# Row clearing, expert weight splitting and the order of the routing work in a four-part transformer block

## The reference

```python
x = x + matmul(fake_quant(norm(x)), fake_quant(ctx))          # 8-bit
x = x + ffn(norm(x))      # 1376 wide; weights rounded in blocks of 32 to 4 bits, activations to 16 bits
x = x + attention(norm(x), ctx)   # 32 query heads, 8 key/value heads of 128; RMS norm on q and k
x = x + moe(norm(x))
```

```python
# moe: 16 experts of 128, two chosen per token, and a shared one of 256
scores = softmax(x @ router_w + router_b) + router_bias
best two groups of four experts, then the best two experts in them; gate = their scores
y  = sum over experts: gate * ((silu(x @ w1 + b1) * (x @ w2 + b2)) @ w3 + b3)
y += (silu(x @ sw1 + sb1) * (x @ sw2 + sb2)) @ sw3 + sb3
```

## Time and profile before

| | |
|---|---|
| Median of 3 runs | 811.12 us (808.1 to 814.69) |
| The profiled execution | 807.26 us, of which the span is 805.4 us |
| PE busy | 647.5 us (80% of the span) |
| DVE | 626.9 us (78%) |
| POOL | 531.1 us (66%) |
| ACT | 494.0 us (61%) |
| Granted TensorE clock, mean | 0.93 of full speed |
| DMA moved | 120.12 MB, mean 149 GB/s |

### The profile page before, as it was taken

How to read it: one execution, slowest core, us unless ns; L and a number is a source line. 1 busy time by engine, 2 the same in 40 slices (tenths; PEclk the granted TensorE clock), 3 DMA queues, 4 the chain that set the end, 5 groups by cost and what they waited for, 6 DMA issues and landing times.

```text
span 805.4 us, 12660 instructions
## 1 busy us (share of the span) xinstructions
PE 647.5 (80%) x3432; PEld 316.6 (39%) x3432; DVE 626.9 (78%) x1331; ACT 494.0 (61%) x986; POOL 531.1 (66%) x505
## 2 busy tenths in 40 slices
PE   0595898846395996999999999999999868676870
PEld 0242343312132442444444444444444335254650
DVE  6896687788899678788888888888888876476622
ACT  4564665659757437777777777777777763145430
POOL 1897586887666557788788888888888744405004
PEclk9899999988688898999999999999999988888995
DMA  8326999992434315877766667666645670499944
GB/s 342 103 81 83 188 188 202 178 166 53 92 59 93 123 58 146 179 169 180 181 142 143 149 156 156 156 143 143 143 92 104 109 244 1 138 289 271 218 145 157
DMA packets 231272, 120.12 MB, mean 149 GB/s; under 512 B 213933, under 2 KB 214189, under 8 KB 228286
## 3 DMA queue, kind: packets, MB, share of 16 engines
q1 hardware_dynamic: 229950, 115.42, 63.3%
q0 software_dynamic: 1280, 4.20, 1.6%
HBM read 57.97 MB, written 15.20 MB: 91 GB/s over the span
## 4 chain that ended last, share of the span: by engine, by line
PE 49%; DVE 20%; DMA 9%; issue 8%; POOL 7%; ACT 4%; SPq 2%; POOLq 0%; DVEq 0%; ACTq 0%
PE ps L1166 16%; PE ps L1168 15%; PE ps L1167 15%; DVE arena L1541 5%; DVE arena L1544 4%; DMA arena<-arena 3%; ACT arena L822 3%; DVE arena L1538 2%; DMA y_d<-arena 2%; POOL arena L594 1%; PE ps L1334 1%; DMA arena<-in_moe_w 1%; POOL arena L586 1%; DVE ss L1691 1%; DMA arena<-in_ffn_w 1%
## 5 line engine op out<-in xcount | busy, mean ns | idle before, releaser
L1166 PE MATMUL ps<-arena 128*128 128x512 f16 (+2 forms) x1011 | 360.6, 361 | 74.2 <-DMA arena<-arena 26.0
L1167 PE MATMUL ps<-arena 128*128 128x512 f16 (+2 forms) x1011 | 359.6, 360 | 0.0
L1168 PE MATMUL ps<-arena 128*128 128x512 f16 (+2 forms) x1011 | 358.6, 359 | 0.0
L822 ACT ACTIVATE arena<-arena 128x512 f16<-128x512 f32 (+8 forms) x404 | 249.2, 649 | 88.1 <-POOL arena L767 29.6
L1166 PEld LDWEIGHTS ps<-arena 128*128 128x128 f16 (+1 forms) x1011 | 102.1, 101 | 191.8 <-issue 51.0
L1538 DVE TENSOR_TENSOR arena<-arena 128x512 f16<-128x512 f32 (+3 forms) x163 | 126.6, 807 | 22.5 <-ACT arena L822 22.2
L1168 PEld LDWEIGHTS ps<-arena 128*128 128x128 f16 (+1 forms) x1011 | 102.5, 101 | 102.2 <-issue 9.8
L1167 PEld LDWEIGHTS ps<-arena 128*128 128x128 f16 (+1 forms) x1011 | 102.3, 101 | 90.4 <-issue 7.2
L767 POOL TENSOR_SCALAR arena<-arena,rden 128x512 f32<-128x512 f32 x128 | 114.5, 894 | 16.1 <-DVE rden L1884 6.8
L1044 ACT ACTIVATE arena<-arena,mneg 128x512 f32<-128x512 f32 x124 | 88.6, 715 | 35.1 <-DVE mneg L1864 35.1
L822 ACT ACTIVATE arena<-ps 128x512 f16<-128x512 f32 (+2 forms) x105 | 58.7, 587 | 52.6 <-PE ps L1168 29.5
(11 more groups left out here) (156 smaller groups left out, 722.5 us busy)
## 6 DMA issues: line engine op xcount, KB each, us to landing
arena<-in_moe_w SPq DMA_DIRECT2D x18, 768.0 KB, 5.5
arena<-in_ffn_w SPq DMA_DIRECT2D x33, 256.0 KB, 6.0
arena<-in_wq SPq DMA_DIRECT2D x8, 1024.0 KB, 5.1
arena<-in_wo SPq DMA_DIRECT2D x8, 1024.0 KB, 5.1
xs_d<-in_ffn_w SPq DMA_DIRECT2D x23, 256.0 KB
y_d<-arena SPq DMA_DIRECT2D x23, 256.0 KB, 3.0
arena<-in_kv_w SPq DMA_DIRECT2D x4, 1024.0 KB, 7.6
arena<-arena SPq DMA_TRANSPOSE x177, 3.3
```

The lines of the kernel that those rows point to most:

```text
L822: return a.activation(out_, in_, ACT.Copy, scale=scale, bias=bias)
L1166: pe.matmul(out_, lhs[0], rhs[0], start=first, stop=False)
L1167: pe.matmul(out_, lhs[0], rhs[1], start=False, stop=False)
L1168: return pe.matmul(out_, lhs[1], rhs[0], start=False, stop=last)
```

## The change

It does five things.

1. The 23 clears leave the chunk loop of SP. They are issued in three runs: seven behind the seventh raw load, eight behind the second key load, eight behind the third.
2. `POOL_LOW` is (0, 1): low parts (and the scaling) of experts 4, 7, 13, 15 and 17 leave POOL, and DVE does all from 2 to 17. Those of 2 to 7 stand behind the routing, beside the shared expert; 8 to 17 in tiles 0 to 9.
3. `ER` = 5. SP's list has the loads up to 12 ahead of the first row load, and load i + 13 in tile i. ACT makes the high part of i + 12 in tile i.
4. The block that prepares biases and the router's weights between steps (7, 1) and (7, 2) is cut into six pieces, which stand in DVE's list ahead of the fourth reciprocal of six steps.
5. The normalised rows get a place of their own (`xe_n`); the order around the routing changes on DVE, ACT and PE.

```diff
-ER = 4
+ER = 5
-POOL_LOW = (0, 1, 4, 7, 13, 15, 17)
+POOL_LOW = (0, 1)
-        xs = [carve(k, (2, D), F16) for k in (36, 38, 190, 192)]
+        xs = [carve(k, (2, D), F16) for k in (36, 38, 150, 152)]
+        xe_n = carve(108, (NT, D))
...
             kw_load(0)
+            def clear(lo, hi):
+                for n in range(lo, hi):
+                    sp.dma_start(blocks[n], blank).then_inc(filled, 16)
             for n in range(RAW):
                 ring(n)
+            clear(0, 7)
             kw_load(1)
+            clear(7, 15)
             ring(RAW)
             kw_load(2)
+            clear(15, TILES)
...
-                if n < TILES:
-                    sp.dma_start(blocks[n], blank).then_inc(filled, 16)
...
             turn_p(HK - 1, 2)
+            load_experts(5)
+            turn_p(HK - 1, 3)
+            sp.wait_ge(a_y, HK * NT - NT)
             load_experts(4)
-            turn_p(HK - 1, 3)
-            for n in range(5, 9):
+            for n in range(6, 13):
                 load_experts(n)
...
-            for n in range(9, 12):
-                load_experts(n)
             for i in range(TILES - XB):
                 x_load(i + XB)
-                if i + 12 < EX:
-                    load_experts(i + 12)
+                if i + 13 < EX:
+                    load_experts(i + 13)
...
 # POOL, behind the last step
-            expert_scale(4)
-            expert_low(4)
-            rstd(6, 0, NT - 1)
-            expert_scale(7)
+            rstd(6, 0, 2)
+            rstd(7, 2, 3)
             for t in range(NT - 1):
                 xs_low(t)
-            rstd(7, NT - 1, NT)
-            expert_low(7)
+            rstd(8, 3, 4)
...
-            for n in (13, 15, 17):
-                expert_scale(n)
-                expert_low(n)
...
 # ACT
             for h in range(R):
-                if h == 2:
-                    expert_high(2)
-                    o_high(last - 1)
                 p_high(last, h)
+            o_high(last - 1)
+            expert_high(2)
             expert_high(3)
-            expert_high(4)
-            expert_high(5)
...
             shared_sigmoid(0)
-            expert_high(8)
+            shared_sigmoid(1)
+            expert_high(5)
+            expert_high(6)
             shared_high(0)
-            shared_sigmoid(1)
+            expert_high(7)
             a.wait_ge(g_t, 1)
             copy(gt[0:NE + 1, 0], bank(0)[0:NE + 1, :]).then_inc(g_c, 1)
             shared_high(1)
+            for n in range(8, 12):
+                expert_high(n)
...
-                if i + 9 < EX:
-                    expert_high(i + 9)
+                if i + 12 < EX:
+                    expert_high(i + 12)
...
 # PE, behind the last tile's transposes
+            pe.wait_ge(m_lo[0], 2)
+            shared_hidden(1, 0, 0, TOK - P)
             pe.wait_ge(h_lo, 2 * NT)
             router(NT - 1, NT)
-            for i in range(2):
-                shared_hidden(0, i, TOK - P, TOK)
-            pe.wait_ge(m_lo[0], 2)
-            shared_hidden(1, 0, 0, TOK)
             pe.wait_ge(r_oh, 1)
             for t in range(NT - 1):
                 earlier(t)
+            shared_hidden(1, 1, 0, TOK - P)
             pe.wait_ge(r_oh, 2)
...
             earlier(NT - 1).then_inc(r_rank, 1)
-            shared_hidden(1, 1, 0, TOK)
+            for n in range(NS):
+                for i in range(2):
+                    shared_hidden(n, i, TOK - P, TOK)
...
 # DVE: a piece of work ahead of a step's fourth reciprocal
                 for h in range(R):
+                    if beside and h == R - 1:
+                        beside()
                     v.wait_ge(a_e, 4 * u + h + 1)
...
                 for h in range(R):
-                    if final and h == 2:
-                        o_low(u - 1)
                     p_low(u, h)
...
-            expert_lows(2)
             stats(0, 2)
-            expert_lows(3)
+            variance(0, 2)
             add_out(HK - 1, 2)
             stats(2, 3)
-            variance(0, 3)
-            for h in range(R):
-                v.wait_ge(turned[h], 16 * HK * NT)
-            expert_norm(6, 0, 3)
+            variance(2, 3)
+            expert_norm(6, 0, 2)
+            expert_norm(7, 2, 3)
...
             choose(0, 3)
             logits(3, 4, 1)
-            (four small operations on iota_1, pick_f, part)
+            mark(0, 3)
             scores(3, 4, 1)
             choose(3, 4)
+            mark(3, 4)
...
+            v.wait_ge(xs_lo, NT)
             shared_hidden(0)
             gates()
+            expert_lows(2)
             shared_low(0)
             shared_hidden(1)
+            expert_lows(3)
             shared_low(1)
-            expert_lows(5)
-            expert_lows(6)
+            (the four small operations)
+            for n in range(4, 8):
+                expert_lows(n)
...
-            beside = {2: 9, 3: 10, 4: 11, 5: 12, 7: 14, 9: 16}
-            tables = {10: extra_tiles, 11: extra_weights}
+            tables = {11: extra_tiles, 12: extra_weights}
...
-                if i == 0:
-                    expert_lows(8)
-                if i in beside:
-                    expert_lows(beside[i])
                 tile_low(i)
+                if i + 8 < EX:
+                    expert_lows(i + 8)
                 if i in tables:
                     tables[i]()
```

More of the change, by code:

```diff
@@ L228, in block_kernel @@
         gsc = carve(165.953125, (NT, 2))
-        xs = [carve(k, (2, D), F16) for k in (36, 38, 190, 192)]
-        xg = [carve(194 + 2 * i, (2 * KD, P), F16) for i in range(XB)]
+        xs = [carve(k, (2, D), F16) for k in (36, 38, 150, 152)]
+        xg = [carve(196 + 2 * i, (2 * KD, P), F16) for i in range(XB)]
+        xe_n = carve(108, (NT, D))
         yb = [carve(k, (D,)) for k in (100, 102, 162)]
@@ L1080, in _ @@
             for h in range(R):
-                if h == 2:
-                    expert_high(2)
-                    o_high(last - 1)
                 p_high(last, h)
+            o_high(last - 1)
+            expert_high(2)
             expert_high(3)
-            expert_high(4)
-            expert_high(5)
             def xs_high(t):
                 a.wait_ge(h_nm, NT + t + 1)
-                copy(xs[t][:, 0], xn[:, t]).then_inc(xs_hi, 1)
+                copy(xs[t][:, 0], xe_n[:, t]).then_inc(xs_hi, 1)
             def xt_high(t):
@@ L1405, in expert_transposes @@
                 for k in range(KD):
-                    mm = pe.transpose(bank(t)[:, k * P:(k + 1) * P], xn[:, t, k * P:(k + 1) * P], ident[:, :])
+                    mm = pe.transpose(bank(t)[:, k * P:(k + 1) * P], xe_n[:, t, k * P:(k + 1) * P], ident[:, :])
                 mm.then_inc(h_ps, 1)
@@ L1890, in attention_step @@
                     tile_low(NT - 1)
-                final = isinstance(j, int) and u == HK * NT - 1
                 for h in range(R):
-                    if final and h == 2:
-                        o_low(u - 1)
                     p_low(u, h)
-                if not final and (not isinstance(j, int) or u >= 1):
+                if not isinstance(j, int) or u >= 1:
                     o_low(u - 1)
@@ L1906, in _, with bias_rows, bias_columns, out_biases @@
             tile_norm(3)
-            for s in range(5):
-                attention_step(0, s)
+            def bias_rows():
+                v.wait_ge(in_mp, 16 * 5)
+                own.mark(v.memset(flat(bias_raw), 0.0))
+                ts(flat(mbs[:, :, :]), flat(mb[:, :, :]), SXW, ALU.mult)
+            def bias_columns():
+                own.mark(v.tensor_copy(bias_raw[:, :, 0:NE], mb[:, :, NS:EX]))
+                v.tensor_copy(bias_raw[:, :, 32:32 + NE], mb[:, :, NS:EX]).then_inc(r_ws, 1)
+            def out_biases():
+                own.mark(ts(b3[0:NE + 1, 0], b3[0:NE + 1, 0], SXW, ALU.mult))
+            def router_scaled():
+                own.mark(ts(flat(rw_raw), flat(rw_raw), SW, ALU.mult))
+                own.mark(v.tensor_reduce(iota, tri, AX.X, ALU.add))
+            def router_high():
+                v.tensor_copy(flat(rw[0]), flat(rw_raw)).then_inc(r_ws, 1)
+                own.mark(ts(later_row, iota, -float(P), ALU.mult, float((NE - 1) * P), ALU.add))
+            def router_low():
+                v.wait_ge(r_ws, 2)
+                tt(flat(rw[1]), flat(rw_raw), flat(rw[0]), ALU.subtract).then_inc(r_ws, 1)
+            attention_step(0, 0)
+            attention_step(0, 1, bias_rows)
+            attention_step(0, 2, bias_columns)
+            attention_step(0, 3, out_biases)
+            attention_step(0, 4, router_scaled)
             def four_steps(j):
@@ L1913, in _ @@
             own.loop(1, HK - 1, 4, four_steps)
[L1914 to L1924, removed]
-            v.tensor_copy(flat(rw[0]), flat(rw_raw)).then_inc(r_ws, 1)
-            v.wait_ge(r_ws, 2)
-            tt(flat(rw[1]), flat(rw_raw), flat(rw[0]), ALU.subtract).then_inc(r_ws, 1)
-            attention_step(HK - 1, 2)
+            attention_step(HK - 1, 1, router_high)
```

(22 more changed lines are left out.)

26 lines of the change are left out of this document (10 added, 16 removed).

## The result

The kernel after takes **817.91 us** (median of 10 runs, 816.36 to 820.88) against 808.5 us for the kernel before (10 runs, 801.9 to 814.69): ratio 1.0125, 95% interval 1.0094 to 1.0155. It is slower, by 1.25%, and outside the range that was predicted. (The forecast was added to 811.12 us, the median of the first three runs of the kernel before; by all ten it is 808.5.) The profiled execution takes 816.80 us (span 814.9) against 807.26; the 9.5 us between them are what the traces have to explain.

The account below looks back on a forecast made before the run. It took the DMA queue in the FFN stage and the stretch from the last attention step to the last expert tile as bounds; -12 - 1.7 + 0.9 = -12.8 us gave 798.3 us from 811.12, range 786 to 811.

Parts of the forecast that it names:

- the front costs nothing: Ahead of the FFN stage, 25 to 68 us: the moved clears fit into 35 us free; bounds 0 and +29 us.
- the near end: Price of one moved clear, taken as a raw load's: 0.77 to about 1.5 us; the far end was 2.8.
- the third rival: Clears pile up ahead of the first weight transpose, 29 us left over: 827 us; decides from 2.1 us a clear; chance 0.09.
- FFN gain: FFN stage: without clears between them, weight transposes land in 3.1 us instead of 5.9; -12 us, range 5 to 18.
- the fifth taken off 14.6 us: FFN stage: discount on the chain's shorter transposes and load, because POOL is next late; leaves -12 us.
- second rival: FFN stage: the clears never cost anything, by the rule on HBM; 810.3 us, chance 0.18.
- Tables: Last attention head group: the preparation block between two steps goes, so DVE's next mean starts earlier; -1.7 us.
- Slots 9.7 earlier: From the last attention step to the routed rows' slots: reordered work makes them ready at 675.2 us, 9.7 earlier.
- Given back: Behind the routing: SP's order holds the row loads, so tile 0's rows land +0.7 us, weight places +0.9.
- terms for two tiles: Expert tiles: one landing, ACT's and DVE's operations and a low part, put at 9.6 us per two tiles.
- first rival: Behind the routing: the early slots are kept, tile 0 starts near 694, tiles gain up to 9; about 789 us, chance 0.15.

Follow-up runs that it names:

- experiment 3: The kernel after, each clear cut into 16 blocks of 8 rows instead of 4 blocks of 32: 793.9 us, ratio 0.9834.
- experiment 6: The kernel before, clears left in the chunk loop but cut into 16 blocks of 8 rows instead of 4 of 32: 795.39 us, ratio 0.9842.
- `A`: The kernel after with clears of 16 blocks of 8 rows, still ahead of the FFN weights: 793.9 us, ratio 0.9834.
- experiment 1: The kernel after, with the 23 clears back in the chunk loop, one behind each of the first 23 weight transposes: 803.68 us, ratio 0.9958.
- Experiments 8 to 10: On `A`: ACT's high part of expert i + 10 in tile i, 786.05 us; loads 10 to 12 behind four row loads, 792.93; both, 781.0.

## Why the prediction was wrong

**The step that failed: "the front costs nothing".** Its term was the price of a clear, taken at the near end, 0.77 to 1.5 us, "since bytes and shape are a raw load's". The bytes are; the shape is not. A raw load's outermost dimension is 128 partitions, the clear's is 4, and that was to be read in two lines that the change leaves as they are (`blank` and `blocks`, L398 and L399 of the kernel before). One of the forecast's own signs of being wrong, a first weight transpose later than 68 us, came at 82.90. Measured, a clear costs 2.44 us, above the 2.1 from which the third rival decides. Its place and mechanism are what happened. Its bound, 2.8 us from "what a transposition was longer for having one ahead", was the better estimate: it came from the only rows in which the clears' cost appeared at all. With the measured price its sum is 23 x 2.44 - 35 = 21 us and 819, or 815.6 on the profiled execution (807.26 - 12.8 + 21.1); measured were 23.9 at the first landing, 817.91 and 816.80.

The chance of 0.09 was the second fault. A gain forecast from the clears' being slow (2.8 us off each transpose) and a cost forecast from their being quick (0.77 to 1.5) can't both stand; experiments 3 and 6 show that they are one quantity. Had the clears been as quick as the front needed, the transposes behind them would not have taken 5.9 us (experiment 6: 3.4), and there would have been little to gain.

**FFN gain: right in size, with a different owner.** Forecast -12; from the first landing to the mask load the kernel after gains 11.5 (23.9 to 12.45), and landings are 3.1. With wide clears `A` keeps 9.8 over experiment 1 (803.68 to 793.9). But experiment 6 gets 12.6 with the clears in the loop: what had to go was their narrowness, not their place. The landings fell as forecast, so the mechanism holds; the fifth taken off 14.6 us was an estimate that no row gave, and that it came so near is in part luck.

**HBM as the bound (second rival): refuted.** 187 GB/s with landings of 3.4 us, against 181 with 5.9 (experiment 6). The Trainium skill's limit of about 358 GB/s per core ("DMA: Bandwidth & Descriptors", section "Where 436 GB/s comes from") was twice what flowed in the FFN stage, so it did not bind, but it did not make the clears free either. By the same page's section "Why a DMA increments its semaphore by 16 and not by 1" the shape was the question, and I had not read it against those two lines.

**Tables: right.** -1.7 forecast; the last step came 1.85 us earlier (+12.45 at the mask load, +10.6 in the last step). Experiments 1 and 3 give the same between these two points, 1.65 and 1.63 us.

**Slots 9.7 earlier: right.** Row numbers went from +10.6 to +1.1, 9.5. The normalisation of tile 3 takes 0.55 us for 3.31, the wait for the rank 1.22 for 3.09.

**Given back: right.** Against the shift of +10.6 the row loads go 3.5 us earlier (forecast 3.6), tile 0 starts 1.1 later (+0.7), the weight places come 0.2 later (+0.9). ACT waits 3.62 us for expert weights in tile 1, as said. (The terms for two tiles add up to 9.5 us, not 9.6; that changes nothing.) Experiments 8 to 10 show the two holders, SP's order and ACT's order, of which ACT's hides SP's: 8 us for ACT's alone (793.9 to 786.05; by the ratios 9), nothing that can be told from `A` for SP's alone, and 5 more for SP's once ACT's is there (786.05 to 781.0, on one chip). The first rival (early slots kept, 789) did not happen, for the reason given against it; SP's place for load 12 was the smaller part of it.

**The sum.** -12 - 1.7 + 0.9 = -12.8 was forecast; measured +23.9 - 11.5 - 1.85 - 1.1 = +9.45 on the profiled execution. Every term but one stands within 2 us. The last, +0.9 forecast for all behind the last step, is -1.1 here, -0.7 in experiment 1 and +2.1 in experiment 3, from single executions, so only that it is small is shown. In experiment 3, where a clear costs what the forecast took it for, the change takes 793.9 us, inside the forecast's own range of 791 to 806.

## What to carry to other kernels

Where a transfer's duration is hidden, look at its outermost dimension on both sides before pricing it by its bytes; a copy with 4 blocks outermost held SP 2.44 us, with 16 or 32 no more than the 0.60 of the issue itself. When a forecast removes a cost in one place and puts the same work elsewhere, use the same price in both. And when a gain is given back, look for two holders in series: undo each alone and both together, for one alone may show nothing.

## What the runs showed of the hardware

- A DRAM-to-DRAM copy of 256 KB with 4 blocks outermost moves at 102 GB/s on a DMA share of 0.26, with 8 at 203 on 0.53, with 16 at 332 on 0.99 (slices of 0.25 us up to 402), with 32 at 348 on 0.96. SP is held 2.44, 0.68, 0.60 and 0.60 us a copy; the last three are near SP's own issue time (0.57 to 0.7 us). The landing of wide clears issued in runs was 5.3 us in the middle, of those standing alone in the loop (experiment 6) 3.6.
- SP is held at the issue while narrow copies are queued, and what is queued goes on: SP was released from the last clear at 82.85 us, and the transpose behind it took 12.24 us to land.
- The granted clock followed the stall: 1.00 from 83 to 95 us before, 0.50 (1.2 of 2.4 GHz) in the kernel after, where PE stood. The first products behind it ran at 0.43 us each, from the eighth on at 0.22 (chain of work of the kernel after):

```profile
97.56 0.43 PE ps L1160
97.99 0.38 PE ps L1158
98.37 0.22 PE ps L1159
```

- Two of POOL's eight scatter issues took longer than the rest in either kernel: 2.42 and 2.12 us after, beside DVE's low parts of 1536 columns; 2.33 and 1.36 us before, beside low parts of 512 columns. The first took 1.26 in both, the others 0.97 to 0.99. All eight together went from 12.0 to 12.8 us. That DVE's work is the cause was not tried. It was not on the path after, since POOL was done 7 us before the row loads went.

```profile
688.61 2.42 POOL L789 DMA_INDIRECT xs_d<-arena,places  x1 [0.31 <-issue]
...
692.62 2.12 POOL L789 DMA_INDIRECT xs_d<-arena,places  x1 [0.31 <-issue]
```
